# Two attention-and-experts layers: the first experts in two token batches, the second attention's norm folded away

## The reference

```python
x = x + attention16(norm(x), ctx, causal)     # 16 heads of 8, biases, Wq Wk Wv Wo
xt = norm(x)                                  # the first experts
w, idx = top_k(softmax(xt @ Wr + br), 2)      # 2 of 16 experts, weights made to sum to 1
h = gelu(einsum('td,edh->teh', xt, W1) + b1)  # 256 hidden
o = einsum('teh,eho->teo', h, W2) + b2
x = x + xt + einsum('teo,te->to', o, comb)    # comb holds w at the chosen experts
x = x + attention2(norm(x), ctx, mask)        # 2 heads of 64: softmax(q k^T / 8) v, Wo, no biases
x = x + experts8(norm(x))                     # top 1 of 8, silu gate, and a shared expert
```

## Time and profile before

| | us |
|---|---|
| median of three runs | 1006.11 |
| profiled execution | 1005.86 |
| its span | 1004.0 |
| opening, to 17.2 | 17.2 |
| first attention with its routing, 17.2 to 396.7 | 379.5 |
| first experts, 396.7 to 553.4 | 156.7 |
| second attention, 553.4 to 748.8 | 195.4 |
| second routing and shared expert, second experts, to the end | 255.2 |
| PE / DVE / ACT / POOL busy in the span | 821.1 / 666.0 / 578.2 / 511.1 |

### The profile page before, as it was taken

The page is one execution under the profiler, slowest core; times in us unless marked ns, Lnnn a source line. Parts: engine busy times, 40 slices in busy tenths (PEclk is TensorE's granted clock), DMA queues, the critical chain, the costliest instruction groups (busy, mean ns, idle before and its releaser), DMA issues. The chain is left out here.

```text
span 1004.0 us, 27974 instructions
## 1 busy us (share of the span) xinstructions
PE 821.1 (82%) x9234; PEld 689.1 (69%) x9234; DVE 666.0 (66%) x2294; ACT 578.2 (58%) x1339; POOL 511.1 (51%) x612
## 2 busy tenths in 40 slices
PE   0699999999999820999998178888858998959997
PEld 0478877878777710999997055555547887849996
DVE  3788899999989742344446379999963546425554
ACT  0588888888888500666665177777756551213332
POOL 4011145555564765344445677777400644726777
PEclk9799999999999855999999599999998999979999
DMA  6000011111116413344332233333213213244441
GB/s 206 11 19 18 14 39 37 47 44 40 49 40 194 143 45 101 112 135 136 131 125 94 72 83 78 82 82 79 55 31 124 85 67 118 107 137 141 145 122 55
DMA packets 67572, 86.33 MB, mean 86 GB/s; under 512 B 22000, under 2 KB 50037, under 8 KB 66960
## 3 DMA queue, kind: packets, MB, share of 16 engines
q1 hardware_dynamic: 47728, 44.71, 15.2%
q0 software_dynamic: 17152, 39.36, 12.1%
q10 hardware_dynamic: 2592, 0.95, 0.5%
HBM read 50.47 MB, written 35.01 MB: 85 GB/s over the span
## 5 line engine op out<-in xcount | busy, mean ns | idle before, releaser
L1155 POOL DMA_INDIRECT f_rows_in<-f_xn_all,f_pos_i x128 | 126.1, 985 | 68.5 <-DVE a_mx L389 34.4
L758 POOL DMA_INDIRECT a_got<-f_rows_out,f_pos_i x128 | 122.7, 958 | 41.5 <-issue 35.4
L1155 POOL DMA_INDIRECT f_rows_in<-f1r_xn_all,f_pos_i x64 | 61.6, 962 | 70.8 <-DVEq L1222 31.3
L1552 POOL DMA_INDIRECT out<-f1e_y,f1e_ids x72 | 76.5, 1062 | 41.3 <-DVE f1e_y L1611 24.7
L1560 POOL DMA_DIRECT2D f_rows_out<-f0e_y x80 | 43.8, 547 | 88.3 <-DVE f0e_y L1614 71.4
L1664 ACT ACTIVATE f0e_hT<-f0e_ps_h,f0e_w 128x256 f32<-128x256 f32 (+1 forms) x160 | 63.8, 449 | 38.5 <-PE f0e_ps_h L1694 38.5
L1614 DVE TENSOR_TENSOR f0e_y<-f0e_ps_y,f0e_w 128x256 f32<-128x256 f32 (+1 forms) x80 | 31.7, 397 | 80.9 <-PE f0e_ps_y L1704 80.6
L618 PE MATMUL a_ps_o<-vx,a_prT 128*64 128x18 f32 x2048 | 83.6, 215 | 2.0 <-DVE x_sb L419 2.0
L618 PEld LDWEIGHTS a_ps_o<-vx,a_prT 128*64 128x64 f32 x2048 | 79.7, 140 | 7.7 <-issue 4.7
L293 POOL TENSOR_TENSOR x_sb<-x_sb,bo 128x256 f32<-128x256 f32 x32 | 23.3, 727 | 116.3 <-DVE a_xn L354 116.0
L389 DVE TENSOR_REDUCE a_mx<-a_ps_s 128x16 f32<-128x1024 f32 x64 | 77.7, 1215 | 5.1 <-PE a_ps_s L589 4.9
(11 more groups left out here) (300 smaller groups left out, 2043.3 us busy)
## 6 DMA issues: line engine op xcount, KB each, us to landing
...
f_rows_in<-f_xn_all,f_pos_i POOLq DMA_INDIRECT x128
```

The costliest lines, as they stand in the source:

```text
L758: pool.indirect_dma_start(got[:, n, k, :], None, N.rows_out[0:N.most, :], bass.IndirectOffsetOnAxis(ap=N.pos_i[:, k, t:t + 1], axis=0)).th ...
L1155: pool.indirect_dma_start(N.rows_in, bass.IndirectOffsetOnAxis(ap=N.pos_i[:, k, t:t + 1], axis=0), self.xn_all[:, t, :], None).then_inc(se ...
L1552: pool.indirect_dma_start(rows_of_out, bass.IndirectOffsetOnAxis(ap=ids[:, n, u:u + 1], axis=0), y[:, n, u, :], None, bounds_check=B * S - ...
```

## The change

- The first two context loads are issued behind the first chunk of x, and the eight later loads move from the opening to the first attention, behind the contexts of its first two groups.
- The first attention routes tiles 0 to 47 only, in six chunks; its last eight groups carry no routing. The slot table of this batch A is made within the last groups. Spare rows of both batches are blanked at its end.
- `first_experts` takes the place of `experts(gated=False)` and is written out slot by slot: batch A has 48 wide and 16 narrow slots, batch B (tiles 48 to 63) 16 wide and 16 narrow. Tiles 48 to 63 are routed between the slots of batch A, at the slot numbers of `NORM_AT` to `BLANK_AT`. SP now loads and stores, a store six slots behind its load, each with its own table load per four slots; before slot 46 it blanks the rows behind the experts' last rows of batch B, with 16 DMAs, and waits until they have landed. POOL adds the normalised rows, sends batch B, and gathers for the second attention the first 18 tiles once batch A's results are stored.
- In the second attention the query weights are multiplied once by (I - 1/C)/8, so that x is transposed as it is; the reciprocal deviation becomes the scale of the exponential, which is split in two, one for each tile. `proj_xk` waits for the adds (`taken`); DVE adds two groups ahead in place of three; `proj_v` stands directly behind `proj_q`; the ring of gathered tiles holds 32.

```diff
+EARLY = 48
+FETCHED = 18
+RING = 16
...
+                    for g in range(2):
+                        sp.dma_start(R.ctxT[:, g, :], A["ctxT"][:, GT * g:GT * (g + 1)]).then_inc(R.ctx_first[g], 16)
...
-            for place, data in later:
-                sp.dma_start(place, data).then_inc(R.later_loaded, 16)
...
-    CHUNKS = [8] * 6 + [4] * 4
+    NG, E, Q = GROUPS, N.experts, N.batches[0]
+    EG = EARLY // 2
+    CHUNKS = [8] * (EARLY // 8)
...
+            for place, data in R.later_loads:
+                sp.dma_start(place, data).then_inc(R.later_loaded, 16)
+            body(1)
+            with sp.Fori(2, NG // 2) as i:
+                body(i)
             K.load_weights(sp, shared=False)
             sp.wait_ge(R.later_loaded, 16 * R.later)
             sp.wait_ge(zeros_made, 1)
+            spares = sum(blank_spare(sp, N, batch, R.zeros[:, :, :], spare_blank) for batch in N.batches)
             K.clear_tails(sp, R.zeros[:, :, :], N.experts // 2)
+            sp.wait_ge(spare_blank, 16 * spares)
+            sp.wait_ge(K.ew_loaded, 16 * K.loads)
...
+            for t in range(sent, EARLY):
+                K.send(pool, t // 8, t, t + 1)
+            pool.wait_ge(K.sent, 16 * EARLY * N.top)
...
+                if i == NG - 2:
+                    K.blocks_by_expert(dve)
+                if i == NG - 1:
+                    K.starts(dve)
...
-    AHEAD = 3
+    AHEAD = 2
...
+            for t in range(FETCHED, TILES):
+                if t >= 2 * RING:
+                    pool.wait_ge(taken, 2 * K * ((t - 2 * RING) // 2 + 1))
+                gather(pool, N, t)
...
-                    dve.tensor_scalar(xn[:, u, :], R.x[:, 2 * G + u, :], mv[:, m, u, 0:1], rstd[:, m, u:u + 1],
-                                      ALU.subtract, ALU.mult).then_inc(xn_ready, 1)
-
+            dve.tensor_scalar(center[:, :], R.ident[:, :], D1 ** -0.5, D1 ** -0.5 / C, ALU.mult, ALU.subtract).then_inc(center_ready, 1)
...
+            dve.wait_ge(centered, 1)
+            dve.tensor_copy(w["wq"][:, :], ps_y[:, 0:P]).then_inc(wq_ready, 1)
...
-                    if within(G + 2, NG):
-                        norm(G + 2, g % 2)
                     if within(G + AHEAD, NG):
-                        add_result(0, *coming)
+                        add_result(0, G + AHEAD)
...
-                        act.activation(pr[:, m, :, :, :], pr[:, m, :, :, :], ACT.Exp, scale=D1 ** -0.5).then_inc(p_ready, 1)
+                        act.wait_ge(rstd_ready, G + 1)
+                        for u in range(2):
+                            last = act.activation(pr[:, m, u, :, :], pr[:, m, u, :, :], ACT.Exp, scale=rstd[:, g, u:u + 1])
+                        last.then_inc(p_ready, 1)
...
-                pe.wait_ge(xn_ready, 2 * G + 2)
+                pe.wait_ge(taken, 2 * K * (G + 1))
...
+                    pe.transpose(ps_xk[:, u * P:(u + 1) * P], R.x[:, 2 * G + u, :], R.ident[:, :])
...
+                        proj_v(G + 1, (g + 1) % NB)
...
-                    if within(G + 1, NG):
-                        proj_v(G + 1, (g + 1) % NB)
...
+    NORM_AT, TURN_AT, LOGITS_AT, BEST_AT, CHOOSE_AT, RANK_AT, READ_AT, PLACE_AT = 11, 12, 13, 22, 26, 27, 28, 29
+    BLOCKS_AT, STARTS_AT, TABLE_AT, TURNED_AT, KEPT_AT, BLANK_AT = 31, 33, 37, 40, 41, 46
+    MOVE_AT = (48, NA + 4)
...
+            for J in range(NS + LAG):
+                if J == BLANK_AT:
+                    K.clear_tails(sp, R.zeros[:, :, :], E)
+                if J == NA:
+                    sp.wait_ge(slots_kept, 1)
+                    sp.wait_ge(K.sent, 16 * 2 * BG * N.top)
+                if J < NS:
+                    Q, j = batch(J)
+                    if j % NB == 0:
+                        rows = table(Q.slot_row[0:1, j:j + NB], mybir.EngineType.SP, Q.spare)
+                    if J >= NB:
+                        sp.wait_ge(xT_done, J - NB + 1)
+                    sp.dma_start(x[:, J % NB, 0:wide(J), :],
+                                 Q.rows_in[bass.ds(rows[j % NB], wide(J) * P), :].rearrange("(p u) c -> p u c", p=P)).then_inc(loaded[J % NB], 16)
+                if J >= LAG:
+                    L = J - LAG
+                    Q, j = batch(L)
+                    if j % NB == 0:
+                        outs = table(Q.slot_out[0:1, j:j + NB], mybir.EngineType.SP, Q.last_out)
+                    sp.wait_ge(y_ready, L + 1)
+                    sp.dma_start(Q.rows_out[bass.ds(outs[j % NB], wide(L) * P), :].rearrange("(p u) c -> p u c", p=P),
+                                 y[:, L % NB, 0:wide(L), :]).then_inc(stored[L % NB], 16)
...
+            for G in range(EARLY // 2):
+                sum_norm(G)
+            pool.wait_ge(ag_done, 1)
+            pool.tensor_scalar(var[:, :], mv[:, :, 1], EPS, None, ALU.add).then_inc(var_ready, 1)
+            pool.wait_ge(var_ready, 1)
+            pool.wait_ge(half_made, 1)
+            pool.tensor_tensor(rstd[:, :], var[:, :], half[:, :], ALU.pow).then_inc(rstd_ready, 1)
+            for v in range(BG):
+                pool.wait_ge(K.kept, v + 1)
+                sum_norm(EARLY // 2 + v)
+            for t in range(EARLY, TILES):
+                K.send(pool, 0, t, t + 1)
+            pool.wait_ge(K.sent, 16 * 2 * BG * N.top)
+            pool.wait_ge(summed, GROUPS)
+            pool.wait_ge(place_link, 3 * N.top)
+            for n in range(NB):
+                pool.wait_ge(stored[n], 16 * (NA // NB))
+            for t in range(FETCHED):
+                gather(pool, N, t)
...
+            for J in range(-LEAD, NS + 1):
+                if 0 < J:
+                    result(J - 1)
+                ahead = J + LEAD
+                if ahead < NS:
+                    Q, j = batch(ahead)
+                    if ahead == NA:
+                        dve.wait_ge(slots_kept, 1)
+                    if j % NB == 0:
+                        e = table(Q.slot_e[0:1, LEAD + j:LEAD + j + NB], mybir.EngineType.DVE, E - 1)
+                    weights(ahead, e[j % NB])
...
-                for n in range(NB):
-                    J, u = NB * i + n, wide(NB * i + n)
-                    pool.wait_ge(y_ready, J + 1)
-                    pool.dma_start(N.rows_out[bass.ds(rows[n], u * P), :].rearrange("(p u) c -> p u c", p=P), y[:, n, 0:u, :]).then_inc(stored[n], 16)
```

More of the change, by code:

```diff
@@ L1017, in body @@
                         proj_xk(G + 2, (g + 2) % NB, i + (g + 2) // NB)
-            rounds(pe, body, NG // NB)
-            body(NG // NB)
+            for i in range(NG // NB + 1):
+                body(i)
 def end_phase(nc, R):
@@ L1243, in starts @@
              dve.scalar_tensor_tensor(self.until[:, :], own[:, 0, :], float(SLOT), start[:, :], ALU.mult, ALU.add))
+    def starts(self, dve):
+        E, N, Q = self.N.experts, self.N, self.Q
+        step = lambda *instructions: self.step(dve, *instructions)
+        start, own, ends = self.start, self.own, self.ends
         a, b, d = own, self.sums, 1
@@ L1481, in experts, with second_experts @@
+def second_experts(nc, A, R, N, out):
+    tag, Q = N.tag, N.batches[0]
+    NS = Q.slots
     W = N.w.shape[2]
     T = SLOT // P
-    H = 2 * FF if gated else FF
-    B1 = H + HALVES * C
-    B2 = B1 + HALVES
+    H = 2 * FF
     with ExitStack() as ctx:
@@ L1512, in wide @@
         def wide(J):
-            return T if not isinstance(J, int) or J < N.pairs else 1
+            return T if not isinstance(J, int) or J < Q.pairs else 1
         def stores(uses):
```

617 lines of the change are left out of this document (387 added, 230 removed).

## The result

The changed kernel took 1041.72 us in the median of four runs (1034.82 to 1045.54) against 1005.48 for the kernel before: a ratio of 1.0338, 95% interval 1.0298 to 1.0378. Run again in a later group it took 1036.01 (1033.06 to 1038.07), ratio 1.0274 [1.024, 1.0309]. It is slower, by 24 to 38 us over both intervals; forecast was 1004, with 980 to 1022 around it. The profiled execution took 1034.82, its span is 1033.1. Why the first four runs lie up to 11 apart stays open; in both groups the longer runs have the lower mean clock (0.950 at 1034.82, 0.935 at 1045.02), except between runs within 0.6 us of each other. What follows goes by profiled executions, and by the ratios where an experiment is judged.

The account below looks back on a forecast made before the run. Four limits: SP's queue in the opening, a routing and send chain ending the first attention, PE in the first experts, a loop of waits in the second attention. 1005.9 - 47.2 + 56.3 - 15.7 + 4.9 = 1004.2; range 980 to 1022.

Parts of the forecast that it names:

- the one up to the result of slot 39: First experts: 87.2 us before, plus late routing on PE and DVE, so slot 39 ends 100.8 after the start.
- together 7.6: First experts, PE: eight pairs of late transposes and logits at some 0.75, and the ranks, cost 7.6 us.
- I take 6, between 0 and 10: First experts, DVE: small routing instructions beyond a slot's slack delay the weight copy PE waits for, 6 us.
- The fourth rival: First experts: late routing not hidden on DVE or PE, small steps stop their slots; another 10, 1014 us; chance 0.13.
- the predicted stall of some 10: First experts: load 46 waits behind SP's 16 zeros and their landing, so PE stalls some 10 us.
- SP's pace: First experts after load 46: two table loads and eight DMAs cost SP 7.04 us per four slots, 1.76 a slot.
- The 1.76 between results in batch B: First experts, a sign of the forecast: SP's queue spaces batch B's results 1.76 us apart.
- The clock rival: First experts' narrow slots: TensorE's clock falls in SP-paced slots, together 10 us more, 1014; chance 0.17.
- The experts' start: End of first attention: the next phase starts at 349.5 instead of 396.7, 47.2 us gained with the opening.
- Its turn: Second attention's loop: PE's transposes wait for DVE's adds, so a turn takes 5.36 us against a mean of 5.15.
- The loss taken for it: Second attention's loop: 30 turns are 160.8 against 154.5, a shorter drain gives 1.4 back; a loss of 4.9 us.
- The one term of 56.3: First experts: a loss of 56.3 us, the phase taking 213.0 against 156.7.

Follow-up runs that it names:

- all four edits: Changed kernel with own PSUM columns per late logits pair, DVE's table load ahead of the result, POOL issuing batch B's zeros, AHEAD = 3: 975.92 us.
- logits and table alone: Changed kernel with own PSUM columns per late logits pair and DVE's table load ahead of the wait for the result: 1015.45 us.
- the chain cut up and eight stores on POOL: All four edits, DVE's late-routing chain cut into pieces over slots 23 to 44, batch A's last eight stores issued by POOL: 968.06 us.
- the table load mended: Changed kernel with DVE's table load of four expert numbers ahead of the wait for a slot's result: 1024.11 us.
- Moving stores to POOL: All four edits, stores of batch A's 16 narrow slots on POOL: 970.48 us; with the chain cut, only the last eight there: 968.06 us.
- the run with AHEAD 3: Changed kernel with AHEAD = 3 in place of 2 in the second attention: 1012.3 us in nine runs.

## Why the prediction was wrong

**The step that failed** is the one up to the result of slot 39 in the first experts: "together 7.6" for PE's late routing and "I take 6, between 0 and 10" for DVE's. The sum had slot 39's result 100.8 after the start of the phase; it came 129.1 after it (475.45 - 346.4), 28.3 late. The instructions were priced and the waits between the two in-order lists were not. Three runs split it. With all four edits, slot 39's result starts 108.4 behind the first x load (127.4 in the kernel after; 106.5 with logits and table alone): 19.0 of the 28.3. With the chain cut up and eight stores on POOL it starts 99.7 behind it, 8.7 less again; with the 1.6 from the phase's start to the first load that is 101.3, near the prediction's 100.8. So the 13.6 for the late routing was about right as a sum. Its two terms are not confirmed apart: of the 13.7 by which that run is behind the kernel before, 3.5 come ahead of slot 13, 4.5 in slots 13 to 21 and 5.7 in slots 21 to 39, with DVE's table loads still among them. The 28 came from where the work stood.

The prediction read DVE's 57 busy us of 134 as slack. It did say that what DVE does in one slot beyond the slack delays the weight copy. It did not ask what PE's new instructions wait for: of every added wait one must name what stands ahead of the signal on the other engine. For the logits that is result, copy and norm, and each of these waits for PE in turn. Nor did it see that the table load moved from ahead of the result to behind it, which the code says and the trace of before cannot show; that DVE's read would take 0.99 in place of 0.35 nothing before the run said. The fourth rival ("the late routing is not hidden at all") named the right place, and its 10 was a third of the size.

**The rest of the first experts.** Load 46 went out 16.3 behind slot 39's result (17.1 predicted), with PE idle for 8.29 and the results 10.0 further apart than a slot: the predicted stall of some 10. Load 46 to 64 took 35.3 (33.1), load 64 to 95 59.2 (53.9), the end 7.1 (8.1). In that 59.2 batch B's wide slots go at 8.95 for four, held by DVE's table load, not at SP's 7.04; with the table load mended they go at 7.8 and the stretch takes 55.9. Together 28.3 - 0.8 + 2.2 + 5.3 - 1.0 = 34.0, the whole difference between 247.0 and 213.0.

**SP's pace** was right where SP set it, in batch A's narrow slots. With all four edits they go at 27.1 / 16 = 1.69, PE waits there for SP's loads, and SP issues every fourth load 7.0 behind the fourth before it, where 7.04 was predicted:

```profile
486.61 0.33 SPq L1552 DMA_DIRECT2D f0e_x<-f0b_rows_in  x1
...
493.66 0.33 SPq L1552 DMA_DIRECT2D f0e_x<-f0b_rows_in  x1
```

The 1.76 between results in batch B, which was to show it, did not come: in the kernel after its wide slots take 2.24 each, its narrow ones 1.41 (568.7 to 591.2 for 16). The sentence from the Trainium skill, DMA: Bandwidth & Descriptors, section Issuing engines are not separate DMA queues, that the sequencer's time is usually small, is no guide for batch A's narrow slots of 64 KB: a store there lands 1.6 us after its issue, longer than the 0.53 of issuing, but two DMAs and a share of two table loads are 1.76 of SP's list, and the slot took 1.19 in the kernel before. Moving stores to POOL still gave 2 us or nothing, because DVE, with 5.5 in the four slots shown, was close behind.

**The clock rival falls.** The windows show 0.87 in slots 13 to 21, where PE was busy 25.42 of 38.00, and 0.94 over the phase. In narrow slots of batch A, where the rival looked for a clock under 0.8, it was 1.00, in the kernel after and with all four edits, though PE waited there again and again for loads (5.7 to 5.8 us in all):

```profile
504.14:532.91 28.77, 19.29 (x148) 17.09 (x147) 14.57 (x38) 14.04 (x48) 0.00 (x0) 1.00 0.29 83
...
471.60:498.70 27.10, 19.17 (x148) 17.06 (x148) 14.68 (x39) 13.99 (x48) 6.30 (x12) 1.00 0.40 117
```

The clock fell with the waits between DVE and PE, and was at 1.00 in slots 21 to 43 when the chain was cut. As far as these windows show, it is a part of their price, not a cause of its own.

**The other steps.** First PE work: 15.5 to 16 predicted, 15.26 measured. The experts' start: 349.5, measured 346.4, a gain of 50.3 where 47.2 was said, with bounds of 44 and 52; SP's list was last there, as predicted (its last zeros went out at 344.13). The second attention's start: 4.2 behind the phase's, measured 4.7. Its turn: 5.36 from six rows of before, measured 5.33, and the run with AHEAD 3 showed that the wait for the adds was the cause. The loss taken for it was still too large: the sum set 5.36, built from one group's rows, beside a mean of 5.15, while that group itself took 5.32 in the kernel before (699.93 to 705.25 in the earlier trace rows); by one and the same mean the turn grew only from 5.25 to 5.33. Without the 34.0 of the first experts the measured time lies 3.4 us under the forecast. The one term of 56.3, which should have been 90.3, decided.

**The range** held neither median. Its top, 1022, had one rival of 10 added to the forecast; the bounds for DVE's term ended at 10, and a round trip between two engines was in none of them.
